# The shared expert of rows 11 to 15 run three steps later, with its input held in emptied staging memory

## The chip, the cores and the metric

The kernel runs on one core of a Trainium2 chip. The metric is the time of one execution in microseconds (us), by the device. Five engines share the core: TensorE (PE in the profile; its weight loads are PEld), VectorE (DVE), ScalarE (ACT), GpSimd (POOL) and SyncE (SP), which here only issues DMAs. Each runs its own list of instructions strictly in the order in which the program wrote it; they meet through semaphores.

## The reference, cut to what matters

The input is 16 rows of 128 tokens with 256 features, and a context of the same shape. Three blocks follow one another, each after a layer norm, each added to its input:

```python
x = x + attention(layernorm(x))                  # 16 heads of 16, rotary, causal
x = x + long_convolution(layernorm(x), ctx)      # 16 kernels as Toeplitz products, gated
x = x + moe(layernorm(x))
# moe: 16 experts of width 176, the best 4 of each token weighted by their softmax;
#      beside them one shared expert of width 704 for every token:
shared = silu(x @ Wg.T) * (x @ Wu.T) @ Wd.T * sigmoid(x @ gate_vec.T)
```

## The kernel before

**Two parts.** In the first part, `NB` = 16 rows go through a software pipeline: attention, convolution, router, choice of slots and shared expert. In it each token's normed input is scattered by four indirect DMAs (POOL, L1518) to the slots of its four experts, in device memory. In the second part, the slot stage, 79 tiles of 128 slots each are loaded, multiplied by their expert's weights (L762, L773, L785, L800) and stored; POOL gathers each token's four results and DVE adds them to the sum that the shared expert left.

**The order.** `ORDER` is written out by hand: for each engine, a list of pieces with how many steps each lies behind. In step s an engine runs, for every piece in its list's order, row s minus that number. On PE a step begins with `px` (the prefix sums that place the slots, behind 5, L640) and ends with `Tk`. `LAST` = 20 is the step in which row 15 gets its slots; in it DVE and POOL take the slot pieces first (`LAST_FIRST`).

**The shared expert's pieces**, by engine. PE: `ga0`, `ga1`, `up0`, `up1` (gate and up products, six matmuls of 352 columns each, L655; `ga0` is behind 4, the others 5), `Th0`, `Th1` (three transposes each, L665) and `dn` (18 matmuls, L677). ACT: `th0`, `th1` (tanh, L943) and `hh0`, `hh1` (L951). DVE: `s10`, `s11` (L1259), `s20`, `s21` (L1269), `hl0`, `hl1` (L1276) and `fin` (L1285), which adds the row's input `x2`. SP stores the sum (`store_shared`, L396). They read the row's normed input transposed, `xT`, and `x2`, both in rings of two buffers.

**Other pieces that the prediction names.** PE: `pt0` to `pt3` (transposes of the probabilities, L540), `at0` to `at3` (probabilities times values, L552), `cv0` to `cv3` (Toeplitz products, L585 and L589), `t2`, `t3`, `t4` (transposes; `t4`, L605, gathers the convolution's parts), `wo`. DVE: `mx` (row maxima, L1085), `gm` (gating of the convolution, L1122), `r1` (L1106). POOL: `kv` and `kl` (products of value and context, and their low half, L1467 and L1479), roots of the layer norms (L1439), scatters.

**Between the parts.** Three small products on PE turn the slot counts into a table of each tile's expert (`table_after`, after `px`, `Th1` and `dn` of step 20). PE then waits for all weights, runs 16 matmuls on zeros (`keep_busy(16, 7)`, L725), waits for the table, and takes the first tile. SP waits for the scatters and then loads eight tiles ahead (L451), after the last `store_shared`.

**Memory and banks.** The eight PSUM banks are used in the fixed turns of `PSUM_ORDER`; `free` waits for the reader of the use before. The weights pass through `stage`, a ring of three units of 1,024 columns, and are split there into high and low half (`PREPARE`, `PREPARE_LO`: the last unit in step 15); in the slot stage the same memory holds results.

Of the kernel before, what the change touches and what calls it, by code (L numbers as in the profile page):

```python
# [6 lines left out]
ALU = mybir.AluOpType  # L7
# [53 lines left out]
DEPTH = 8  # L61
# [54 lines left out]
def build(nc, x, ctx_in, w_units, w_route, bias, skip, trig, causal, ident, masks, ecol, iota, out):  # L116
    stack = ExitStack()
    with stack:
# [85 lines left out]
        cws = ring("shared_weight", 2, [P, 1])  # L204
# [48 lines left out]
        bhh = [st[:, 2240 + n * E:2240 + (n + 1) * E] for n in range(2)]  # L253

# [83 lines left out]

        def free(pe, use, row):

            b, i = HOME[use]
            line = BANKS[b]
            step = row + int(line[i][1])
            for back in range(1, 3 * len(line) + 1):
                n = i - back
                u, behind = line[n % len(line)]
                r = step + n // len(line) - int(behind)
                if 0 <= r < NB:
                    sig, k = READER[u]
                    sig.wait(pe, r, k)  # L350
                    return
                if step + n // len(line) < 0:
                    return
# [30 lines left out]
        def _(sp):  # L384
# [90 lines left out]
        def _(pe):  # L475
# [141 lines left out]
            def router(row):  # L617
                xT_lo.wait(pe, row)
                if row == 0:
                    pe.wait_ge(s_const_lo, 1)  # L620
                free(pe, "ro", row)
                n = 0
                for kc in range(KC):
                    for a in range(2):
                        for b in range(2):
                            last = nc.tensor.matmul(bank("ro")[:, 0:NR], xT[a][row % 2][:, kc, :], wr[b][:, kc, :],
                                                    start=n == 0, stop=n == 7)
                            n += 1
                last.then_inc(routed.sem, 1)
# [17 lines left out]
            def half_product(c, side, use, ready):  # L647
                def piece(row):
                    xT_lo.wait(pe, row)
                    if row == 0:  # L650
                        pe.wait_ge(s_w_lo, U_GU)
                    free(pe, use, row)
                    for kc in range(KC):
                        for a, b, first, end in products(kc == 0, kc == KC - 1):
                            last = nc.tensor.matmul(bank(use)[:, 0:CH], xT[a][row % 2][:, kc, :],  # L655
                                                    sgu[b][:, c, kc, side, :], start=first, stop=end)
                    last.then_inc(ready.sem, 1)
                return piece
# [73 lines left out]
            for s in range(NB + DEPTH):  # L732
                if s == 1:
                    pe.wait_ge(s_once, 4)
                for name, behind in ORDER["PE"]:
                    if 0 <= s - behind < NB:
                        pieces[name](s - behind)
                    if s - behind == NB - 1 and name in table_after:
# [11 lines left out]
            emptied(7)  # L750
            keep_busy(16, 7)
# [60 lines left out]
        def _(act):  # L812
# [102 lines left out]
            def moe_x_hi(row):  # L915
                xn3_T.wait(act, row)
                up_ready.wait(act, row - 2)
                nc.scalar.activation(xT[0][row % 2][:].rearrange("p c n -> p (c n)"), bank("xT")[:, 0:E], ACT.Copy)\
                    .then_inc(xT_hi.sem, 1)
# [40 lines left out]
            def first_use(row):  # L960
# [10 lines left out]
                "vT": copy_vT, "nm3": normalise(2, lambda row: x2[row % 2], scattered), "xh": moe_x_hi,  # L971
# [6 lines left out]
            for s in range(NB + DEPTH):  # L978
                if s == 1:
                    act.wait_ge(s_const, NCONST)  # L980
                    nc.scalar.activation(wr[0][:], wr_f[:], ACT.Copy, scale=WS).then_inc(s_const_hi, 1)
                    act.wait_ge(s_bias, 32)
                    nc.scalar.activation(brow[:], stage[:, RING - 1, :], ACT.Copy, scale=WS).then_inc(s_const_hi, 1)
                for n, (name, behind) in enumerate(ORDER["ACT"]):
                    for u in PREPARE.get((s, n), ()):
                        split_unit(u)
                    if 0 <= s - behind < NB:
                        pieces[name](s - behind)
# [35 lines left out]
        def _(dve):  # L1024
# [101 lines left out]
            def residual2(row):  # L1126
                o2_T.wait(dve, row)
                normed[2].wait(dve, row - 2)
                xsh_ready.wait(dve, row - 2)
                nc.vector.scalar_tensor_tensor(out=x2[row % 2][:], in0=bank("o2T")[:, 0:E], scalar=1.0 / WS,  # L1130
                                               in1=x1[row % 2][:], op0=ALU.mult, op1=ALU.add).then_inc(x2_ready.sem, 1)

            def moe_x_lo(row):
                xT_hi.wait(dve, row)
                nc.vector.tensor_tensor(xT[1][row % 2][:].rearrange("p c n -> p (c n)"), bank("xT")[:, 0:E],
                                        xT[0][row % 2][:].rearrange("p c n -> p (c n)"), ALU.subtract)\
                    .then_inc(xT_lo.sem, 1)

            def shared_weight(row):
                gth_done.wait(dve, row)  # L1140
                nc.vector.tensor_scalar(cws[row % 2][:], gth[row % 2][:], 1.0, 0.5 * SILU, ALU.add, ALU.mult)\
# [121 lines left out]
            def shared_up(c):  # L1263
                def piece(row):
# [4 lines left out]
                    nc.vector.scalar_tensor_tensor(out=hh[c][:, 0:CH], in0=bank(f"up{c}")[:, 0:CH], scalar=cws[row % 2][:],  # L1269
# [11 lines left out]
            def shared_out(row):  # L1281
                down_done.wait(dve, row)
                if row >= 2:
                    dve.wait_ge(s_xsh[row % 2], 16 * (row // 2))
                nc.vector.scalar_tensor_tensor(out=xsh[row % 2][:], in0=bank("dn")[:, 0:E], scalar=1.0 / WS,  # L1285
                                               in1=x2[row % 2][:], op0=ALU.mult, op1=ALU.add).then_inc(xsh_ready.sem, 1)
# [40 lines left out]
            table_after = {"ix": round_tiles, "hl1": mark_tiles, "fin": copy_table}  # L1327
            s_set = sem("buffers_set")
            for n in range(2):
# [18 lines left out]
                       (lambda row: x2[row % 2], lambda row: x2_ready.wait(dve, row)))  # L1348
# [7 lines left out]
            for s in range(NB + DEPTH):  # L1356
# [14 lines left out]
                for n, (name, behind) in enumerate(order("DVE", s)):  # L1371
                    for u in PREPARE_LO.get((s, n), ()):
                        split_unit(u)
                    if 0 <= s - behind < NB:
                        pieces[name](s - behind)
                    if s - behind == NB - 1 and name in table_after:
                        table_after[name]()
# [56 lines left out]
        def _(pool):  # L1434
# [117 lines left out]

            conv_ready.wait(pool, NB - 1)
# [103 lines left out]
```

## Time and profile before

| | |
|---|---|
| Time, median of 3 runs | 626.28 us (625.69 to 627.07) |
| Span of the profiled execution (first to last instruction) | 671.6 us |
| Mean granted clock of TensorE in it | 0.975 |
| Busy in the span: PE, DVE, ACT, POOL | 89%, 74%, 62%, 59% |

The profiled execution's own time is known only by its span, which is 45 us above the median of the runs without the profiler. An instruction counts as busy from its start to its end; matmuls overlap, and their ends are modelled, so a PE that is busy all through a stretch need not be at its peak in it. The granted clock is 1.00 at 2.4 GHz and 0.50 at 1.2 GHz. In the first part a step of the steady pipeline takes about 24.4 us. In the profile's time, step 16 begins on PE at 359.32, step 17 at 383.70, step 18 at 407.40, step 19 at 424.36 and step 20 at 433.88; the slot stage's first transpose starts at 450.59.

### The profile page before, as it was taken

The numbers are of one execution on the slowest core, as the hardware profiler recorded it, in microseconds if no ns is written. First come the engines' busy times: TensorE is split into PE (matmuls) and PEld (weight loads), VectorE is DVE, ScalarE is ACT, GpSimd is POOL, SyncE is SP. The second block draws the span as 40 slices with busy tenths as digits, with TensorE's granted clock in tenths as the row PEclk, the third lists the DMA queues.
The fourth block names the chain that finished last, engine by engine and source line by source line (L and its number), as shares of the span: only waits on it lengthen the run. The fifth ranks groups of instructions, "written<-read, shape, count | busy, mean of one in ns | idle before, by whom it ended". The sixth has DMA issues, their size and how long they took to land.

```text
span 671.6 us, 18614 instructions
## 1 busy us (share of the span) xinstructions
PE 597.1 (89%) x5901; PEld 464.0 (69%) x5901; DVE 495.8 (74%) x1516; ACT 414.5 (62%) x1060; POOL 394.7 (59%) x439
## 2 busy tenths in 40 slices
PE   8888999999999999999999998869998787878670
PEld 3567877888988878988988886636765455556450
DVE  4567797898898888998778667557766666767672
ACT  3877886787687687787677563216655454545440
POOL 1156768788888778778888778530023434343442
PEclk9999999999999999999999989979998989989996
DMA  6825422324432422532112100234455646555442
GB/s 181 288 86 174 144 74 86 124 75 135 128 91 85 126 77 100 158 96 89 38 52 79 50 12 31 72 117 126 128 141 155 180 146 185 166 178 166 147 125 90
DMA packets 55680, 78.93 MB, mean 118 GB/s; under 512 B 7330, under 2 KB 46370, under 8 KB 55588
## 3 DMA queue, kind: packets, MB, share of 16 engines
q1 hardware_dynamic: 37300, 48.51, 23.9%
q0 software_dynamic: 6912, 18.88, 9.3%
q10 hardware_dynamic: 11376, 10.36, 4.5%
q8 instruction: 52, 0.85, 0.5%
q14 instruction: 40, 0.33, 0.2%
HBM read 44.43 MB, written 33.29 MB: 116 GB/s over the span
## 4 chain that ended last, share of the span: by engine, by line
PE 73%; issue 8%; POOL 5%; ACT 4%; DVE 3%; another core or an unknown queue 2%; DMA 1%; ACTq 1%; SPq 1%; POOLq 0%; DVEq 0%
PE ps L773 10%; PE ps L655 8%; PE ps L552 7%; PE ps L585 5%; PE ps L486 5%; PE ps L677 5%; PE ps L785 4%; PE ps L605 4%; PE ps L796 3%; PE ps L540 3%; PE ps L589 3%; PE ps L762 2%; PE ps L523 2%; PE ps L513 2%
## 5 line engine op out<-in xcount | busy, mean ns | idle before, releaser
L1549 POOL DMA_INDIRECT toeplitz_lo<-y_slots,slots x44 | 42.4, 963 | 111.6 <-DMA y_slots<-stage 71.8
L773 PE MATMUL ps<-w_gate_up_hi,toeplitz_hi 128*128 x316 | 85.7, 319 | 14.6 <-DVE toeplitz_hi L1388 14.6
L1479 POOL TENSOR_TENSOR kv_lo<-kv,kv_hi 128x512 f16<-128x512 f32 x64 | 77.6, 1212 | 30.6 <-ACT kv_hi L911 30.3
L1518 POOL DMA_INDIRECT x_slots<-x_norm,slots x64 | 70.5, 1102 | 19.7 <-issue 14.9
L1467 POOL TENSOR_TENSOR kv<-ctx_t_sb,v_t 128x512 f32<-128x512 f32 x64 | 68.9, 1086 | 11.9 <-ACT v_t L900 9.5
L880 ACT ACTIVATE probs<-ps,row_neg_max 128x128 f32<-128x128 f32 x256 | 71.6, 390 | 3.4 <-DVE row_neg_max L1085 3.3
L552 PEld LDWEIGHTS ps<-v_ones,probs_t 128*128 128x128 f32 x512 | 62.2, 192 | 2.2
L1388 DVE TENSOR_TENSOR toeplitz_hi<-ps,toeplitz_hi 128x256 f16<-128x256 f32 x79 | 33.4, 423 | 40.1 <-ACT toeplitz_hi L994 38.8
L552 PE MATMUL ps<-v_ones,probs_t 128*128 128x17 f32 x512 | 60.7, 256 | 0.0
L585 PE MATMUL ps<-kv_hi,toeplitz_hi 128*128 128x128 f16 x256 | 56.6, 221 | 3.4 <-POOL kv_lo L1479 1.8
L994 ACT ACTIVATE toeplitz_hi<-ps 128x256 f16<-128x256 f32 x79 | 30.3, 383 | 45.3 <-ACT stage L1013 15.1
L1439 POOL TENSOR_TENSOR ln_rstd<-ln_var,minus_half 128x1 f32<-128x1 f32 x48 | 30.4, 634 | 46.7 <-DVE ln_var L1040 46.6
L585 PE MATMUL ps<-kv_hi,toeplitz_lo 128*128 128x128 f16 x256 | 56.4, 220 | 0.0
L585 PE MATMUL ps<-kv_lo,toeplitz_hi 128*128 128x128 f16 x256 | 56.4, 220 | 0.0
L1122 DVE TENSOR_TENSOR conv_gated<-ps,ctx_t_sb 128x512 f32<-128x512 f32 x64 | 43.7, 683 | 15.3 <-PE ps L589 15.0
L773 PEld LDWEIGHTS ps<-w_gate_up_hi,toeplitz_hi 128*128 128x128 f16 x316 | 31.3, 99 | 29.4 <-issue 17.4
L773 PE MATMUL ps<-w_gate_up_lo,toeplitz_hi 128*128 x158 | 50.2, 318 | 0.0
L589 PE MATMUL ps<-kv_hi,toeplitz_lo 128*128 128x64 f16 x256 | 49.6, 194 | 0.0
L589 PE MATMUL ps<-kv_lo,toeplitz_hi 128*128 128x64 f16 x256 | 49.6, 194 | 0.0
L589 PE MATMUL ps<-kv_hi,toeplitz_hi 128*128 128x64 f16 x256 | 49.6, 194 | 0.0
L1085 DVE TENSOR_REDUCE row_neg_max<-ps 128x4 f32<-128x512 f32 x64 | 43.2, 681 | 6.5 <-PE ps L529 6.5
L911 ACT ACTIVATE kv_hi<-kv 128x512 f16<-128x512 f32 x64 | 40.1, 626 | 9.7 <-PE ps L589 6.9
(226 smaller groups left out, 2099.1 us busy)
## 6 DMA issues: line engine op xcount, KB each, us to landing
stage<-in_w_units SPq DMA_DIRECT2D x36, 512.0 KB, 3.7
x_slots<-zeros SPq DMA_DIRECT2D x15, 512.0 KB
toeplitz_hi<-x_slots SPq DMA_DIRECT2D x40, 128.0 KB, 2.3
y_slots<-stage ACTq DMA_DIRECT2D x40, 128.0 KB, 2.3
y_slots<-kv ACTq DMA_DIRECT2D x39, 128.0 KB, 2.1
kv_hi<-x_slots SPq DMA_DIRECT2D x20, 128.0 KB, 2.7
x_slots<-zeros SPq DMA_DIRECT2D x1, 2432.0 KB
kv_lo<-x_slots SPq DMA_DIRECT2D x19, 128.0 KB, 2.2
```

Of the source, the lines that this page charges most:

```text
L552: last = nc.tensor.matmul(bank("av")[:, h * (HD + 1):(h + 1) * (HD + 1)], pT[g % 2][:, s, :], v_sb[row % 2][:, h, :], start=True, stop=Tru ...
L585: nc.tensor.matmul(to, toep_w[a][:, QUADS * g + h, 0, :], kvh[b][g % 2][:, h, :, :].rearrange("p c n -> p (c n)"), start=first, stop=end, ...
L589: last = nc.tensor.matmul(to[:, 64:128], toep_w[a][:, QUADS * g + h, 1, :], kvh[b][g % 2][:, h, 0, :], start=first, stop=end, skip_group_c ...
L655: last = nc.tensor.matmul(bank(use)[:, 0:CH], xT[a][row % 2][:, kc, :], sgu[b][:, c, kc, side, :], start=first, stop=end)
L773: last = nc.tensor.matmul(psum[2 + t % 2][:, 0:2 * INTER], bxT[a][t % 2][:, kc, :], egu[b][:, bass.ds(e, 1), kc, :].rearrange("p a n -> p ...
L880: last = nc.scalar.activation(sm[g % 2][:, s, :], bank(f"sc{g}")[:, s * P:(s + 1) * P], ACT.Exp, bias=mx[row % 2][:, g, s:s + 1])
L1085: nc.vector.tensor_reduce(mx[row % 2][:, g, :], bank(f"sc{g}")[:].rearrange("p (s n) -> p s n", n=P), X, ALU.max, negate=True).then_inc(ma ...
L1122: nc.vector.tensor_tensor(to, y, cT.broadcast_to([P, QUADS, KC, SIDE, SIDE]), ALU.mult)\
L1467: nc.gpsimd.tensor_tensor(kv[g % 2][:], cs.broadcast_to([P, SIDE, SIDE, SIDE]), vs.broadcast_to([P, SIDE, SIDE, SIDE]), ALU.mult).then_inc ...
L1479: nc.gpsimd.tensor_tensor(flat(kvh[1][g % 2]), kv[g % 2][:].rearrange("p h j i -> p (h j i)"), flat(kvh[0][g % 2]), ALU.subtract).then_inc ...
L1518: pool.indirect_dma_start(out=xbuf, out_offset=bass.IndirectOffsetOnAxis(ap=slots[:, row, j:j + 1], axis=0), in_=xn[2][row % 2][:], in_off ...
L1549: pool.indirect_dma_start(out=yg[n][j], out_offset=None, in_=ybuf[0:(last_tile(row) + 1) * P], in_offset=bass.IndirectOffsetOnAxis(ap=slot ...
```

## The change

Rows 0 to 10 stay as they were. The shared pieces of rows 11 to 15 run three steps later than their place in the lists gives: for a piece that lies b behind, steps b+11 to b+13 have none, and steps b+14 to b+18 take rows 11 to 15. The loop gets two more steps, in which (steps 21 to 23 on PE) only shared pieces of rows 13 to 15 are left. Their inputs are kept until then: `x2` and `xT` of those rows are written into `stage`, 512 columns a row. The 16 matmuls on zeros go.

```diff
-DEPTH = 8
+DEPTH = 10
+HELD, HOLD = 11, 3
+SHARED_PIECES = frozenset("ga0 ga1 up0 up1 Th0 Th1 ih0 ih1 dn th0 th1 hh0 hh1 s10 s11 s20 s21 hl0 hl1 fin store_shared".split())
+def due(name, behind, step):
+    row = step - behind
+    if name not in SHARED_PIECES or row < HELD:
+        return row
+    return row - HOLD if row >= HELD + HOLD else -1
...
-        cws = ring("shared_weight", 2, [P, 1])
+        cws = ring("shared_weight", 8, [P, 1])
...
+        def held(row, lo, hi):
+            at = 2 * E * (row - HELD)
+            return st[:, at + lo:at + hi]
+        def x2_of(row):
+            return x2[row % 2][:] if row < HELD else held(row, 0, E)
+        def xT_of(half, row):
+            if row < HELD:
+                return xT[half][row % 2][:]
+            return held(row, E + P * half, E + P * (half + 1)).bitcast(F16).rearrange("p (c n) -> p c n", c=KC)
+        def held_free(eng, row):
+            eng.wait_ge(s_w_lo, UNITS - RING + 1 + 2 * E * (row - HELD) // UNIT)
...
+        TURNS = [sorted((step, i, u, due(u, int(behind), step)) for i, (u, behind) in enumerate(line)
+                        for step in range(NB + DEPTH) if 0 <= due(u, int(behind), step) < NB) for line in BANKS]
+        BEFORE = {now[2:]: last[2:] for turns in TURNS for last, now in zip(turns, turns[1:])}
         def free(pe, use, row):
...
+            if (use, row) in BEFORE:
+                u, r = BEFORE[use, row]
+                sig, k = READER[u]
+                sig.wait(pe, r, k)
...
-                    row = s - behind
-                    if 0 <= row < NB and not (name == "load_x" and row < 3) and not (name == "load_ctx" and row < 2):
+                    row = due(name, behind, s)
+                    if 0 <= row < NB and not (name == "load_x" and row < 3) and not (name == "load_ctx" and row < 2) \
+                            and not (name == "store_shared" and row >= HELD + 2):
                         pieces[name](row)
...
             for t in range(NX):
                 load_tile(t)
+            for row in range(HELD + 2, NB):
+                store_shared(row)
...
             pe.wait_ge(s_w_lo, UNITS)
-            emptied(7)
-            keep_busy(16, 7)
             pe.wait_ge(s_table, 1)
...
             def moe_x_hi(row):
                 xn3_T.wait(act, row)
-                up_ready.wait(act, row - 2)
+                if row < HELD:
+                    up_ready.wait(act, row - 2)
+                else:
+                    held_free(act, row)
...
             def gate_th(t):
                 t_gu.wait(act, t)
                 t_ga.wait(act, t - 2)
+                if t == 0:
+                    up_ready.wait(act, NB - 1)
+                    xsh_ready.wait(act, NB - 1)
...
             def residual2(row):
                 o2_T.wait(dve, row)
-                normed[2].wait(dve, row - 2)
-                xsh_ready.wait(dve, row - 2)
+                if row < HELD:
+                    normed[2].wait(dve, row - 2)
+                    xsh_ready.wait(dve, row - 2)
+                else:
+                    held_free(dve, row)
...
-            table_after = {"ix": round_tiles, "hl1": mark_tiles, "fin": copy_table}
+            table_after = {(LAST, "ix"): round_tiles, (LAST, "hl1"): mark_tiles, (LAST + 1, "fin"): copy_table}
...
+            xsh_ready.wait(pool, NB - 1)
             conv_ready.wait(pool, NB - 1)
```

Every other edited line passes the row through `due`, `x2_of` or `xT_of`; on PE the three products of the table stay in step 20.

## Rows read from the trace of the kernel before

**Rows 1.** The page: the span, and the chain that ended last, by engine.

```profile
span 671.6 us, 18614 instructions
...
PE 73%; issue 8%; POOL 5%; ACT 4%; DVE 3%; another core or an unknown queue 2%; DMA 1%; ACTq 1%; SPq 1%; POOLq 0%; DVEq 0%
```

**Rows 2.** Windows: length, busy us of PE, PEld, DVE, ACT, POOL; granted clock, DMA.

```profile
359.32:383.70 24.38, 24.38 (x290) 20.72 (x287) 17.76 (x59) 16.77 (x44) 19.41 (x22) 1.00 0.18 60
383.70:407.40 23.70, 23.69 (x267) 20.19 (x265) 16.44 (x52) 14.35 (x39) 16.19 (x20) 0.93 0.11 34
407.40:424.36 16.96, 13.66 (x180) 11.21 (x177) 11.66 (x40) 5.86 (x14) 15.34 (x19) 1.00 0.10 36
424.36:433.88 9.52, 7.52 (x66) 5.11 (x63) 7.11 (x33) 3.28 (x9) 4.66 (x7) 1.00 0.21 71
433.88:447.13 13.25, 8.77 (x57) 5.95 (x55) 6.82 (x34) 1.64 (x4) 5.71 (x8) 0.74 0.20 71
447.13:450.59 3.46, 3.46 (x18) 1.62 (x17) 1.56 (x9) 0.00 (x0) 0.94 (x2) 1.00 0.49 159
...
480.00:500.00 20.00, 20.00 (x151) 14.19 (x150) 14.41 (x51) 13.29 (x40) 1.87 (x2) 1.00 0.47 129
```

**Rows 3.** Timeline of PE: start us, us, line, shapes; around the shared products.

```profile
366.19 0.53 PE L665 MATMUL ps<-identity,inner 128*128 128x128 f32 x3
...
434.11 0.31 PE L655 MATMUL ps<-w_shared_gate_up_hi,moe_x_t_hi 128*128 128x352 f16 x1
...
436.64 0.31 PE L655 MATMUL ps<-w_shared_gate_up_hi,moe_x_t_lo 128*128 128x352 f16 x1
...
450.59 0.38 PE L762 MATMUL ps<-identity,toeplitz_hi 128*128 128x128 f32 x2
```

**Rows 4.** Chain of waits: start us, us, what; `dn` of rows 13, 15.

```profile
420.56 1.97 PE ps L677 x18
...
443.01 4.02 PE ps L677 x18
```

**Rows 5.** Timelines of DVE and POOL, steps 17, 18; in brackets the idle before.

```profile
386.86 0.51 DVE L1259 SCALAR_TENSOR_TENSOR gate_th<-gate_th,ps 128x352 f32<-128x352 f32 x1
387.29 1.28 DVE L1085 TENSOR_REDUCE row_neg_max<-ps 128x4 f32<-128x512 f32 x2
...
398.68 0.26 DVE L1092 RECIPROCAL softmax_recip<-ps 128x16 f32<-128x16 f32 x1 [1.66 <-PE ps L552]
...
403.47 0.41 DVE L1106 SCALAR_TENSOR_TENSOR x<-ps,x_sb 128x256 f32<-128x256 f32 x1
...
420.65 0.69 DVE L1122 TENSOR_TENSOR conv_gated<-ps,ctx_t_sb 128x512 f32<-128x512 f32 x1 [1.19 <-PE ps L589]
...
404.84 0.57 POOL L1439 TENSOR_TENSOR ln_rstd<-ln_var,minus_half 128x1 f32<-128x1 f32 x1 [0.36 <-DVE ln_var L1040]
...
408.20 2.09 POOL L1467 TENSOR_TENSOR kv<-ctx_t_sb,v_t 128x512 f32<-128x512 f32 x2 [0.27 <-issue]
```

**Rows 6.** POOL's groups, 360 to 420 us: busy, mean ns | idle before, releaser.

```profile
L1479 POOL TENSOR_TENSOR kv_lo<-kv,kv_hi 128x512 f16<-128x512 f32 x12 | 13.8, 1151 | 7.9 <-ACT kv_hi L911 7.9
L1467 POOL TENSOR_TENSOR kv<-ctx_t_sb,v_t 128x512 f32<-128x512 f32 x12 | 12.6, 1061 | 1.0 <-issue 0.5 <-ACT v_t L900 0.5
L1518 POOL DMA_INDIRECT x_slots<-x_norm,slots x9 | 9.7, 1074 | 2.3 <-issue 2.3
...
L1506 POOL TENSOR_TENSOR slot_weight_of<-slot_hit,expert_weight 128x64 f32<-128x64 f32 x2 | 0.6, 320 | 1.9 <-issue 1.8
```

**Rows 7.** Timelines of ACT, DVE and SP from step 20 on.

```profile
441.24 0.49 ACT L951 ACTIVATE inner_t_hi<-ps 128x384 f16<-128x384 f32 x1 [4.39 <-issue]
...
439.66 1.07 DVE L1269 SCALAR_TENSOR_TENSOR inner<-ps,shared_weight,gate_th 128x352 f32<-128x352 f32 x2
...
441.76 1.20 DVE L1276 TENSOR_TENSOR inner_t_lo<-ps,inner_t_hi 128x384 f16<-128x384 f32 x2 [1.03 <-ACT inner_t_hi L951]
...
447.95 1.81 SPq L451 DMA_DIRECT2D toeplitz_hi<-x_slots  x4
```

More of the change, by code:

```diff
@@ L625, in router @@
                         for b in range(2):
-                            last = nc.tensor.matmul(bank("ro")[:, 0:NR], xT[a][row % 2][:, kc, :], wr[b][:, kc, :],
+                            last = nc.tensor.matmul(bank("ro")[:, 0:NR], xT_of(a, row)[:, kc, :], wr[b][:, kc, :],
                                                     start=n == 0, stop=n == 7)
@@ L654, in piece @@
                         for a, b, first, end in products(kc == 0, kc == KC - 1):
-                            last = nc.tensor.matmul(bank(use)[:, 0:CH], xT[a][row % 2][:, kc, :],
+                            last = nc.tensor.matmul(bank(use)[:, 0:CH], xT_of(a, row)[:, kc, :],
                                                     sgu[b][:, c, kc, side, :], start=first, stop=end)
@@ L735, in _ @@
                 for name, behind in ORDER["PE"]:
-                    if 0 <= s - behind < NB:
-                        pieces[name](s - behind)
-                    if s - behind == NB - 1 and name in table_after:
+                    if 0 <= due(name, behind, s) < NB:
+                        pieces[name](due(name, behind, s))
+                    if s == LAST and name in table_after:
                         table_after[name]()
@@ L916, in moe_x_hi @@
                 xn3_T.wait(act, row)
-                up_ready.wait(act, row - 2)
-                nc.scalar.activation(xT[0][row % 2][:].rearrange("p c n -> p (c n)"), bank("xT")[:, 0:E], ACT.Copy)\
+                if row < HELD:
+                    up_ready.wait(act, row - 2)
+                else:
+                    held_free(act, row)
+                nc.scalar.activation(xT_of(0, row).rearrange("p c n -> p (c n)"), bank("xT")[:, 0:E], ACT.Copy)\
                     .then_inc(xT_hi.sem, 1)
@@ L970, in _ @@
                 "hi2": lhs2, "nm2": normalise(1, lambda row: x1[row % 2], lambda row: v_T.wait(act, row - 1)),
[L971 removed]
+                "vT": copy_vT, "nm3": normalise(2, x2_of, scattered), "xh": moe_x_hi,
                 "gt": gate_tanh, "lg": logits, "re": router_exp,
@@ L986, in _ @@
                         split_unit(u)
-                    if 0 <= s - behind < NB:
-                        pieces[name](s - behind)
+                    if 0 <= due(name, behind, s) < NB:
+                        pieces[name](due(name, behind, s))
             def x_hi(t):
@@ L1140, in shared_weight @@
                 gth_done.wait(dve, row)
-                nc.vector.tensor_scalar(cws[row % 2][:], gth[row % 2][:], 1.0, 0.5 * SILU, ALU.add, ALU.mult)\
+                nc.vector.tensor_scalar(cws[row % 8][:], gth[row % 2][:], 1.0, 0.5 * SILU, ALU.add, ALU.mult)\
                     .then_inc(cws_done.sem, 1)
@@ L1268, in piece @@
                     inner_T.wait(dve, row - 1, c + 1)
-                    nc.vector.scalar_tensor_tensor(out=hh[c][:, 0:CH], in0=bank(f"up{c}")[:, 0:CH], scalar=cws[row % 2][:],
+                    nc.vector.scalar_tensor_tensor(out=hh[c][:, 0:CH], in0=bank(f"up{c}")[:, 0:CH], scalar=cws[row % 8][:],
                                                    in1=th[c][:], op0=ALU.mult, op1=ALU.mult).then_inc(inner_done.sem, 1)
@@ L1347, in _ @@
             sources = ((lambda row: x_sb[row % 3], x_ready), (lambda row: x1[row % 2], lambda row: x1_ready.wait(dve, row)),
-                       (lambda row: x2[row % 2], lambda row: x2_ready.wait(dve, row)))
+                       (x2_of, lambda row: x2_ready.wait(dve, row)))
             for n, (src, ready) in enumerate(sources):
@@ L1373, in _ @@
                         split_unit(u)
[L1374 to L1377, printed above, removed]
+                    if 0 <= due(name, behind, s) < NB:
+                        pieces[name](due(name, behind, s))
+                    if (s, name) in table_after:
+                        table_after[s, name]()
             for n in range(2):
```

21 lines of the change are left out of this document (4 added, 17 removed).

## The prediction

> **What bounds the kernel now.** I read the chain of waits first: 73% of the span is PE's [rows 1], so PE's time is the price of most things. Then windows cut where a step begins on PE. The first number behind the length is PE's busy time. In steps 16 and 17 PE is busy throughout (24.38 of 24.38, 23.69 of 23.70); in step 18 it is busy 13.66 of 16.96 while POOL has 15.34; in steps 19 and 20 nothing is full: PE has 7.52 of 9.52 and 8.77 of 13.25, the latter at a granted clock of 0.74 [rows 2]. The slot stage then has a PE busy for 20.00 of 20.00 again, so a late start of it is paid in full. From the first transpose at 450.59 [rows 3] to the end of the span lie 671.6 - 450.6 = 221 us that the change doesn't touch. So the question is one date: when does the slot stage start?
>
> A busy PE is not yet a bound. POOL has 19.41 of step 16's 24.38 us [rows 2], and most of what is left is its waiting [rows 6]. The pipeline runs close to two bounds; taking work off one lets it shorten only as far as the other.
>
> **What the moved work costs on PE.** 18 gate and up matmuls start between 434.11 and 436.64, 0.149 us apart [rows 3]; 24 a row make 3.6 us. Two groups of three transposes take 0.53 each with the tail of the last [rows 3], some 0.4 to the next instruction: 0.8. `dn` takes 1.97 [rows 4]. Together 6.3 us a row.
>
> **Steps 16 to 18: three rows' products leave.** If PE alone set the pace, 3 x 6.3 = 18.9 us would go. I follow the waits instead.
>
> Step 17: `s11` leaves DVE ahead of the row maxima (386.86, the maxima at 387.29 [rows 5]). The exponentials and `pt0` need the maxima, so `up0` and `up1`, which filled that wait, yield some 0.5, not 1.8. `Th0`, `Th1` between the transposes: 0.8. `ga0` lay beside the reciprocal, which waited 1.66 for PE [rows 5], and the output's normalisation: 0.5. `dn` lay beside the chain residual (403.47), root of the layer norm on POOL (404.84), two scatters, next products (408.20) [rows 5], which keeps its 4.7 us: nothing. At a clock of 0.93 [rows 2], 0.07 x 23.7 x 2 = 3.3 us ran at 1.2 GHz and cost at most half of that; with PE no longer the bound I take 1.2 as recovered. Sum 3.0.
>
> Step 16: 0.5 and 0.8 as above, nothing for `ga0` and the clock (1.00), and 0.8 for `dn`, which there outlasts the layer norm: 2.1. Step 18: POOL runs almost without a gap from 408.20 until row 15's last `kl`; 0.3 of waiting goes. `dn` (420.56, 1.97 [rows 4]) then lay between `cv3` and `t4`; but `t4` must wait for the gating (420.65, 0.69 [rows 5]), so 1.1 of it goes: 1.4.
>
> Sum of the gains: 2.1 + 3.0 + 1.4 = 6.5 us. Bound above: all waiting of POOL between 360 and 420 that others cause goes, 7.9 + 1.0 + 1.9 = 10.8 [rows 6] (the 2.3 between scatters follow their own issue and stay), and all of `dn`, 2.0: 12.8. Bound below: a loss of 1, if a thinner PE gets step 17's clock in step 16 too and nothing else moves. I take 6.5; the nearest row is step 18, where PE already had 3.3 us free and POOL set the length.
>
> **Steps 19 and 20: other rows, same work.** Rows 11 and 12 stand where 14 and 15 stood, in the same places of each list, also behind DVE's slot pieces in step 20. New is `ga0` of row 13 between the table's second product and `dn`: 0.9 us, 1.8 at 1.2 GHz (`dn` took 4.02 there instead of 1.97 [rows 4]), against some 1.1 in which `dn` (443.01 [rows 4]) waited for `hl1` (441.76 and 1.20 on [rows 7]): +0.7, bounds 0 and 1.8.
>
> **Steps 21 to 23: the three rows come back, ahead of the first tile.** PE is in order, so the first tile waits for `dn` of row 15. A row's cycle: `ga1`, `up0`, `up1` 2.7 us, with tanh (no row shows it here; as long as `hh`, 0.49 [rows 7]), `s11` 0.5 and `s20` beside them; `Th0`, then `Th1` behind `s21` (a pair takes 1.07 [rows 7]), at 3.9; the next row's `ga0` beside `hh1` 0.49 and `hl1` 0.6 [rows 7], at 5.1; `dn` 2.0: 7.1. Three rows: 21.3 us from the end of the table's products. Bound below: no idle, 3 x 6.3 less the `ga0` counted in step 20: 18.0. Above: step 19's pace, 9.5 [rows 2]: 28.5.
>
> What hides there: the 3.5 us from 447.13 to 450.59 [rows 2]. The 16 matmuls on zeros that go filled exactly those, but what PE waited for was data, the first tile's load being issued at 447.95 [rows 7]; so dropping them saves nothing beyond these 3.5. The loads land long before `dn` of row 15, which spares the first tiles' waits: 0.8 (bounds 0 and 1.5, estimated; no row of its own).
>
> **Waits and queues.** SP issues the stores of rows 11 and 12, then the eight loads, then three stores; `fin` of row 15 needs only row 13's store, done some 7 us before. `gate_th` of tile 0 now waits for `fin` of row 15, due half a us after `dn`; `gate_up` of that tile ends later; behind it in ACT's list stand tile 1's pieces, which need PE anyway. POOL's gathers queue behind a wait for the same `fin`, and need stored tiles, far later. `held_free` asks for weight units split by step 15, before row 13 needs them: nothing. Deeper `cws`, other addresses, fewer ring waits: nothing queued on those. If a cover fails, the stage starts later by that wait, at most 2 us.
>
> **Sum.** -6.5 + 0.7 + 21.3 - 3.5 - 0.8 = +11.2: the span goes from 671.6 to 682.8 us. The span is 45 us over the median of the runs shown; I don't know where that time lies, but the terms are lengths of the first part's work, so I put the difference on the median: 626.28 + 11.2 = 637.5 us.
>
> **The rivals.**
>
> *PE is the bound after all (faster).* For it: PE is busy 100% of steps 16 and 17. Then 18.9 go and the 1.2 of clock: -20.1 + 17.7 = -2.4, 623.9 us. The place is POOL: its waits for ACT's `kv_hi` [rows 6] would have to vanish and its own work shrink. It turns at a gain of 17.7, above the bound of 12.8. Chance 0.10.
>
> *POOL runs without waiting (slower by less).* -12.8 + 17.7 = +4.9, 631.2; with rows 13 to 15 dense as well (18.0), +1.6, 627.9. For it: PE is what `kv_hi` waits for in the end. Against: `kl3` waits for `pt3`, behind an exponential chain that stays. Chance 0.13; its lower end touches no change.
>
> *The clock falls in steps 16 to 18.* The granted clock was 0.93 in step 17 although PE was busy throughout, and 0.74 in step 20 [rows 2]. What leaves is plain matmuls; transposes stay. At 0.74 over the 65.0 - 6.5 = 58.5 us then left, 0.26 x 58.5 = 15.2 us of PE time are lost; PE has about that much idle there, so I put half on the path: +7.6, 645.1. The Trainium skill, "TensorE: Matmul & The Clock Gate", part 4 on the transpose mode, says that a transpose doesn't count as PE activity the way a matmul does; by it, step 17's dip with a full PE is what a step rich in transposes gives, and this rival gains weight. Against, by the rows: step 16 has the same transposes at 1.00. Chance 0.09.
>
> *Rows 13 to 15 take step 19's pace.* 28.5 instead of 21.3: +7.2, 644.7. For it: step 20 takes 13.25 for one row. Against: both steps hold the router's chain and slots, which these three lack. Chance 0.08.
>
> **How the numbers follow.** The forecast has 0.60, with its own range of 632 to 642 (gain 2 to 10, cycles of 6.7 to 7.6). About 0.2%, 1.25 us, is what a measurement tells from no change. Faster: 0.10, the first rival. Within 0.2%: 0.06, the second's dense end and what lies between the two. Slower: 0.84. The range 628 to 645 leaves out the first rival, the second's last edge and half of the last two: under 0.2.
>
> **What would show it.** In the profile after: step 16 about 22 us long, 17 about 20.5, 18 about 15.5, POOL's share in them up, PE's below 85%; row 15's `px` near 427.4; three groups of 24 L655, 6 L665 and 18 L677, about 7 us apart, before the first L762 near 461.8; no L725 there; the stage still 221 us. A first L762 at or before 450.6 makes the forecast wrong: then PE set steps 16 to 18. If it comes near 469, the clock or the last rows' waits were mis-sized.

## The result, and the profile after

The kernel after takes 647.85 us (median of 4 runs, 643.0 to 650.14), the kernel before in the same job 625.99 us (625.16 to 627.07): ratio 1.0363 [1.0324, 1.0402], 21.9 us slower. The forecast was slower by 11.2 us, with a range that ended at 645.

One thing must be put right before the profiles are compared. The execution of before that is shown ahead of the prediction was not like the others: its 671.6 us are 45 over the runs, and what disturbed it is not known. A second profile of before was therefore taken (first experiment), and in this part "before" is that profile wherever no group of rows is named. Windows of it, cut where row 11's to row 15's prefix product starts on PE and at the first transpose of the slot stage (length, busy us of PE, PEld, DVE, ACT, POOL, granted clock, DMA):

```profile
358.51:382.89 24.38, 24.38 (x290) 20.72 (x288) 17.74 (x58) 16.77 (x44) 18.89 (x22) 1.00 0.16 55
382.89:404.90 22.01, 22.01 (x266) 19.12 (x264) 15.46 (x53) 14.37 (x39) 16.03 (x20) 1.00 0.11 35
404.90:421.73 16.83, 13.68 (x180) 11.21 (x178) 12.54 (x41) 5.86 (x14) 15.29 (x19) 1.00 0.12 42
421.73:429.97 8.24, 7.26 (x66) 5.19 (x64) 6.85 (x32) 3.28 (x9) 4.58 (x7) 1.00 0.20 66
429.97:443.77 13.80, 10.01 (x73) 5.93 (x71) 8.32 (x42) 1.64 (x4) 6.68 (x10) 1.00 0.34 112
```

The same cuts in the kernel after, where the last window but one ends with the table's products and the last holds rows 13 to 15:

```profile
357.44:379.67 22.23, 19.21 (x241) 16.20 (x239) 14.89 (x51) 15.61 (x40) 18.07 (x21) 1.00 0.18 59
379.67:405.91 26.24, 21.18 (x219) 18.97 (x216) 15.39 (x46) 12.83 (x35) 16.27 (x19) 0.80 0.06 22
405.91:425.98 20.07, 13.00 (x137) 11.33 (x136) 11.84 (x35) 4.59 (x11) 15.71 (x19) 0.66 0.08 27
425.98:434.23 8.25, 7.27 (x66) 5.18 (x64) 6.85 (x32) 3.19 (x9) 4.72 (x7) 1.00 0.19 66
434.23:442.95 8.72, 7.20 (x63) 4.86 (x60) 7.03 (x34) 2.10 (x5) 5.70 (x8) 1.00 0.30 106
442.95:464.95 22.00, 19.22 (x141) 13.31 (x141) 11.29 (x26) 5.27 (x11) 0.32 (x1) 1.00 0.21 67
```

The chain of waits is PE's still, with 77% of the span (80% in before, 73% in the shown profile [rows 1]):

```profile
span 646.2 us, 18581 instructions
...
PE 77%; issue 6%; POOL 6%; DVE 4%; ACT 3%; DMA 2%; SPq 1%; POOLq 0%; DVEq 0%; ACTq 0%
```

The slot stage starts 21.18 us later (464.95 against 443.77) and then lasts as long as before (646.2 - 464.95 = 181.2; 625.2 - 443.77 = 181.4). So all of the loss is one date, as the prediction had it. It is made up of: -1.07 before step 16 (0.99 of it stands already at step 14, ahead of the first piece that was moved, so it parts the two executions and not the kernels), -2.15 in step 16, **+4.23 in step 17, +3.24 in step 18**, +0.01 in step 19, +16.92 from step 20's start to the stage. The end was forecast at +17.7. Steps 16 to 18 were to give 6.5 back and took 5.3 more.

The three rows at the end, PE's timeline (the first `dn` matmul of rows 13 and 14, the first transpose of the stage; compare [rows 3, 4]):

```profile
448.37 0.28 PE L702 MATMUL ps<-w_shared_down_hi,inner_t_hi 128*128 128x256 f16 x1 [0.28 <-DVE inner_t_lo L1308]
...
455.67 0.28 PE L702 MATMUL ps<-w_shared_down_hi,inner_t_hi 128*128 128x256 f16 x1 [0.28 <-DVE inner_t_lo L1308]
...
464.95 0.60 PE L785 MATMUL ps<-identity,toeplitz_hi 128*128 128x128 f32 x4
```

and in before, the matmuls on zeros and the first transpose of the stage:

```profile
438.78 3.63 PE L725 MATMUL ps<-zeros 128*128 128x512 f16 x16
443.77 0.41 PE L762 MATMUL ps<-identity,toeplitz_hi 128*128 128x128 f32 x2 [1.36 <-DMA toeplitz_hi<-x_slots]
```

A row's cycle is 7.30 us with 0.6 of idle, and the first tile's transpose no longer waits for its load, as it did for 1.36 us in before.

What stands in steps 17 and 18 is seen on DVE. The scan that numbers the tiles, 128 x 16 elements, in the kernel after (start, us, engine, line, operation; first step 17, then step 18):

```profile
380.41 3.67 DVE L1234 TENSOR_TENSOR_SCAN tile_newest<-ones_f,tile_newest,tile_opened 128x16 f32<-128x16 f32 x1
...
384.41 0.68 DVE L1114 TENSOR_REDUCE row_neg_max<-ps 128x4 f32<-128x512 f32 x1
...
406.64 3.85 DVE L1234 TENSOR_TENSOR_SCAN tile_newest<-ones_f,tile_newest,tile_opened 128x16 f32<-128x16 f32 x1
```

and POOL beside it:

```profile
380.81 2.10 POOL L1499 TENSOR_TENSOR kv<-ctx_t_sb,v_t 128x512 f32<-128x512 f32 x2
382.86 1.16 POOL L1511 TENSOR_TENSOR kv_lo<-kv,kv_hi 128x512 f16<-128x512 f32 x1
384.43 0.57 POOL L1471 TENSOR_TENSOR ln_rstd<-ln_var,minus_half 128x1 f32<-128x1 f32 x1 [0.41 <-DVE ln_var L1069]
...
407.24 2.10 POOL L1499 TENSOR_TENSOR kv<-ctx_t_sb,v_t 128x512 f32<-128x512 f32 x2
409.29 1.15 POOL L1511 TENSOR_TENSOR kv_lo<-kv,kv_hi 128x512 f16<-128x512 f32 x1
```

In before the scan of step 17 took 0.24 us (that of step 18 0.99):

```profile
383.62 0.24 DVE L1202 TENSOR_TENSOR_SCAN tile_newest<-ones_f,tile_newest,tile_opened 128x16 f32<-128x16 f32 x1
...
383.89 1.00 DVE L1207 TENSOR_TENSOR tile_ahead<-tile_newest,tile_end 128x16 f32<-128x16 f32 x1
...
383.80 2.09 POOL L1467 TENSOR_TENSOR kv<-ctx_t_sb,v_t 128x512 f32<-128x512 f32 x2 [0.69 <-ACT v_t L900]
385.86 1.14 POOL L1479 TENSOR_TENSOR kv_lo<-kv,kv_hi 128x512 f16<-128x512 f32 x1
```

Read the ends. The scan after ends at 384.08 and 410.49, just when POOL's unbroken run of kv, kv, kv_lo has ended (384.02, 410.44). POOL then stands still for 0.41 us, waiting for a layer norm piece that itself queued on DVE behind the scan. In before POOL waited 0.69 us for `v_t` first, and the scan slipped in at 383.62. One thing the records leave open: the held scans are recorded 0.40 and 0.60 us ahead of the first kv, and a free one, 0.23 us long, would have been over by then. What shut them out began before POOL's product is recorded. The row maxima queue behind the scan; PE's next transposes wait for them. The chain of waits has the scan on it, and PE's timeline shows the holes:

```profile
380.49 3.59 DVE tile_newest L1234
```

```profile
386.42 0.45 PE L565 MATMUL ps<-identity,probs 128*128 128x128 f32 x1 [2.81 <-ACT probs L903]
...
410.50 0.29 PE L610 MATMUL ps<-kv_hi,toeplitz_hi 128*128 128x128 f16 x1 [4.32 <-POOL kv_lo L1511]
```

The granted clock goes to 0.50 in these holes, which is 1.2 GHz of 2.4, and PE's work runs at that pace for 10.2 and 13.7 us:

```profile
385.54:395.78 10.24, 9.37 (x90) 9.33 (x91) 4.03 (x13) 6.03 (x19) 5.34 (x7) 0.50 0.00 1
409.43:423.08 13.65, 10.62 (x112) 9.11 (x112) 6.46 (x19) 3.52 (x9) 10.88 (x13) 0.50 0.03 11
```

The second hole is not the scan's: PE waits there for POOL's `kv_lo`. In before 18 gate and up matmuls (2.84 us) lay in it and 1.17 us of idle was left.

### The profile page after: what moved, and what is told of

Its sections match the earlier page's. It is cut to its first block, busy times and chain, and to the rows that moved or that the text cites. A ratio compares the mean times of both kernels' runs of the same rounds, so it can differ in the third digit from the quotient of the medians.

```text
span 646.2 us, 18581 instructions
## 1 busy us (share of the span) xinstructions
PE 592.7 (92%) x5885; PEld 465.1 (72%) x5885; DVE 499.4 (77%) x1516; ACT 417.4 (65%) x1060; POOL 396.8 (61%) x439
## 4 chain that ended last, share of the span: by engine, by line
PE 77%; issue 6%; POOL 6%; DVE 4%; ACT 3%; DMA 2%; SPq 1%; POOLq 0%; DVEq 0%; ACTq 0%
PE ps L796 11%; PE ps L680 9%; PE ps L577 7%; PE ps L610 6%; PE ps L702 5%; PE ps L511 5%; PE ps L808 4%; PE ps L819 4%; PE ps L565 4%; PE ps L630 3%; PE ps L614 3%; PE ps L785 3%; POOL kv_lo L1511 2%; PE ps L548 2%; PE ps L538 2%
## 5 line engine op out<-in xcount | busy, mean ns | idle before, releaser
L1511 POOL TENSOR_TENSOR kv_lo<-kv,kv_hi 128x512 f16<-128x512 f32 x64 | 80.4, 1257 | 35.5 <-ACT kv_hi L934 35.2
L796 PE MATMUL ps<-w_gate_up_hi,toeplitz_hi 128*128 x316 | 83.7, 313 | 1.0 <-DVE toeplitz_hi L1420 1.0
L1550 POOL DMA_INDIRECT x_slots<-x_norm,slots x64 | 69.0, 1077 | 19.1 <-issue 14.8
L610 PE MATMUL ps<-kv_hi,toeplitz_hi 128*128 128x128 f16 x256 | 58.4, 228 | 6.2 <-POOL kv_lo L1511 5.8
L610 PE MATMUL ps<-kv_hi,toeplitz_lo 128*128 128x128 f16 x256 | 58.7, 229 | 0.0
L610 PE MATMUL ps<-kv_lo,toeplitz_hi 128*128 128x128 f16 x256 | 58.7, 229 | 0.0
L614 PE MATMUL ps<-kv_hi,toeplitz_hi 128*128 128x64 f16 x256 | 51.2, 200 | 0.0
L915 ACT ACTIVATE probs_t<-ps 128x512 f32<-128x512 f32 x64 | 39.0, 613 | 10.9 <-PE ps L565 10.7
```

The lines of the kernel that those rows point to most:

```text
L610: nc.tensor.matmul(to, toep_w[a][:, QUADS * g + h, 0, :], kvh[b][g % 2][:, h, :, :].rearrange("p c n -> p (c n)"), start=first, stop=end, ...
L614: last = nc.tensor.matmul(to[:, 64:128], toep_w[a][:, QUADS * g + h, 1, :], kvh[b][g % 2][:, h, 0, :], start=first, stop=end, skip_group_c ...
L796: last = nc.tensor.matmul(psum[2 + t % 2][:, 0:2 * INTER], bxT[a][t % 2][:, kc, :], egu[b][:, bass.ds(e, 1), kc, :].rearrange("p a n -> p ...
L1511: nc.gpsimd.tensor_tensor(flat(kvh[1][g % 2]), kv[g % 2][:].rearrange("p h j i -> p (h j i)"), flat(kvh[0][g % 2]), ALU.subtract).then_inc ...
L1550: pool.indirect_dma_start(out=xbuf, out_offset=bass.IndirectOffsetOnAxis(ap=slots[:, row, j:j + 1], axis=0), in_=xn[2][row % 2][:], in_off ...
```

## The experiments

Three theories. **P**: DVE's small operations with two operands in SBUF are shut out while POOL's products run on; in steps 17 and 18 that makes PE late and idle. **C**: PE's clock falls because the shared products left. **B**: POOL or one row's chain sets these steps, so nothing was to be had. What all runs gave, in us of their one profile (cuts as above), and the time as a ratio to before, which was timed anew beside each group of runs. A profile is one execution; those of D, E and one row are of the fastest run of their kernel, that of D again of the slowest.

| kernel | 16 | 17 (clock) | 18 (clock) | less than before, 16 to 18 | ratio |
|---|---|---|---|---|---|
| before | 24.38 | 22.01 (1.00) | 16.83 (1.00) | | |
| after | 22.23 | 26.24 (0.80) | 20.07 (0.66) | -5.3 | 1.0363 [1.0324, 1.0402] |
| A, late kv0 | 22.23 | 23.62 (0.86) | 17.18 (0.80) | +0.2 | 1.0274 [1.0216, 1.0332] |
| B, filler | 23.44 | 23.28 (0.93) | 20.04 (0.74) | -3.5 | 1.0349 [1.0311, 1.0387] |
| D, scan in PSUM | 22.23 | 20.17 (1.00) | 17.25 (0.80) | +3.6 | 1.0248 [1.0215, 1.0281] |
| D again | 23.41 | 23.36 (0.85) | 17.27 (0.80) | -0.8 | 1.0273 [1.0242, 1.0305] |
| E, D and filler | 22.23 | 20.64 (1.00) | 18.02 (0.91) | +2.3 | 1.0270 [1.0236, 1.0305] |
| G, D and hole filled | 22.23 | 20.18 (1.00) | 19.85 (0.83) | +1.0 | 1.0252 [1.0224, 1.0279] |
| one row | 22.31 | 23.81 (1.00) | 16.82 (1.00) | +0.3 | 1.0088 [1.0053, 1.0122] |
| one row, scan in PSUM | 22.31 | 21.91 (1.00) | 16.83 (1.00) | +2.2 | 1.0034 [1.0011, 1.0058] |

**The kernel before, again** (no edit).

> The kernel before once more, for a second profile of it. In the profile shown the slot stage lasted 221 us, in the kernel after 181.2 us (465.0 to 646.2), though the change leaves that stage alone. If the profile of before was disturbed there, its stage now takes 172 to 182 us and the first transpose of it again lies near 450.6. A stage near 174 would mean that some 7 us of the 21.9 lost lie in the stage itself; a stage near 181 would mean that the first part of the kernel before is shorter than its profile showed, by some 7 us.

Measured: span 625.2, stage 181.4, first transpose at 443.77. So the stage is as long as after's, and the shown profile was too long in its first part as well, by 6.8 us: 1.7 in step 17, 1.3 in step 19, 2.9 from step 20 on, in a stretch with a granted clock of 0.74 [rows 2], where `dn` took 4.02 us [rows 4] against 2.15 here, 0.8 before step 16 and 0.1 in step 18.

**A: POOL's first products later.**

```
 # POOL, first value products of a row
+if row in (14, 15):
+    page_step.wait(pool, row - 2, 3)      # scan and lookup of the row two before are done
```

> The kernel after, but POOL begins the value products of rows 14 and 15 only when DVE has done the scan and the tile lookup of the row two before. Theory P (the scan, 3.67 and 3.85 us instead of 0.23, is held by POOL's unbroken run of products; PE then stands idle, and its clock falls for that): the scan takes 0.2 to 1 us in steps 17 and 18, the granted clock there is 0.9 or more, and the time falls by 8 to 12 us against the kernel after, to 636 to 640. Theory C (the clock falls because plain matmuls left these steps, whatever the scan does): the scans are short but the clock stays at 0.80 and 0.66, and the time falls by 3 us at most. Theory B (POOL or the chain of one row sets the length of these steps in any case): scans short, clock up, time down by less than 3.

```profile
380.46 0.23 DVE L1234 TENSOR_TENSOR_SCAN tile_newest<-ones_f,tile_newest,tile_opened 128x16 f32<-128x16 f32 x1
...
385.06 0.41 PE L565 MATMUL ps<-identity,probs 128*128 128x128 f32 x2 [1.16 <-ACT probs L903]
...
408.01 0.29 PE L610 MATMUL ps<-kv_hi,toeplitz_hi 128*128 128x128 f16 x1 [4.39 <-POOL kv_lo L1513]
...
404.98 0.87 DVE L1264 SCALAR_TENSOR_TENSOR slot_key<-picked,slot_place 128x16 f32<-128x16 f32 x1
```

The scans are short (0.23 in both steps), PE's wait in step 17 falls from 2.81 to 1.16, and steps 17 and 18 give back 2.62 and 2.89 us. But the clock still falls, at 385.79, and steps 17 and 18 run at 0.86 and 0.80. POOL's products begin only 0.3 us later for it (381.13 against 380.81 in the same step). The time is 643.60 us; the ratio goes down by 0.9%, 5.6 us, between what P and C expected: the hold is real, and it isn't all. This run is also the nearest to one without holds: no DVE operation of its steps 16 to 18 takes over 1.13 us (`slot_key` 0.87). Yet steps 16 to 18 give 0.2 us in its profile where 6.5 were forecast.

**B: the clock alone.** In steps 16 to 18 PE multiplies zeros where the shared products stood.

```
+FILL = {"up1": 10, "ga0": 2, "dn": 3}    # matmuls on zeros, s in (16, 17, 18)
+elif name in FILL and s in (16, 17, 18):
+    fill(name, s)
```

> The kernel after, but in steps 16 to 18 PE does matmuls on zeros where the shared products stood (10 at the place of up1, 2 of ga0, 3 of dn), whose results nobody reads. Theory C (the clock falls for want of plain matmuls): clock back at 0.95 to 1.00 in steps 17 and 18, the time 5 to 8 us below the kernel after. Theory P: the scans still last 3.6 us, clock up in part, the time down by 4 us or less. Theory B: no change within 1.5 us either way.

```profile
382.81 3.67 DVE L1244 TENSOR_TENSOR_SCAN tile_newest<-ones_f,tile_newest,tile_opened 128x16 f32<-128x16 f32 x1
...
382.08:405.36 23.28, 21.51 (x233) 17.14 (x231) 15.84 (x46) 12.58 (x35) 16.29 (x19) 0.93 0.07 24
405.36:425.40 20.04, 14.89 (x150) 11.46 (x149) 12.81 (x35) 4.59 (x11) 15.69 (x19) 0.74 0.08 28
```

The clock comes back in part, the scan stays held, step 17 gains 3.0, step 16 loses 1.2 to the filler, and the time, 647.17 us, does not move outside its interval; C's 5 to 8 us are missed; theories P and B had both allowed for this. Filling in zeros alone is not the way out.

**D: the hold alone.** For rows 12 and 13 the scan reads its second operand from PSUM and writes there, and the lookup reads it there; POOL's work stays where it was.

```
# shortened
+tensor_scalar(px[:, 48:64], px[:, 0:16], ...)             # the opened tiles, in PSUM too
-tensor_tensor_scan(newest, ones_f, opens, start, ...)     # both inputs in SBUF
+tensor_tensor_scan(px[:, 64:80], ones_f, px[:, 48:64], start, ...)
-tensor_tensor(ahead, newest, tile_end, subtract)
+tensor_copy(newest, px[:, 64:80]); tensor_tensor(ahead, px[:, 64:80], tile_end, subtract)
```

> The kernel after, but for rows 12 and 13 the scan takes its opened tiles from PSUM and leaves its result there, and the tile lookup reads it there, so that each has one operand in SBUF instead of two; POOL's work is not moved. If POOL's products shut these two out because both of their operands lie in SBUF, the scan takes 0.3 us at most in steps 17 and 18 and the lookup too, PE's idle of 2.81 and 4.32 us shrinks, step 17 comes to 23 to 24 us and step 18 to 16 to 17.2, and the time falls by 4 to 7 us against the kernel after, to 641 to 644; a clock that still falls in step 17 would then be a second, separate cost (theory C). If the scan was late for another reason (its semaphores, DVE's queue), it still takes some 3.7 us and nothing changes.

```profile
379.74 0.24 DVE L1239 TENSOR_TENSOR_SCAN ps<-ones_f,tile_newest,ps 128x16 f32<-128x16 f32 x1
...
380.10 0.16 DVE L1252 TENSOR_TENSOR tile_ahead<-ps,tile_end 128x16 f32<-128x16 f32 x1
...
380.06 2.10 POOL L1512 TENSOR_TENSOR kv<-ctx_t_sb,v_t 128x512 f32<-128x512 f32 x2
...
400.88 2.78 DVE L1277 SCALAR_TENSOR_TENSOR slot_key<-picked,slot_place 128x16 f32<-128x16 f32 x1
...
378.92:399.09 20.17, 16.77 (x219) 14.61 (x217) 11.84 (x48) 12.48 (x35) 16.27 (x19) 1.00 0.08 28
399.09:416.34 17.25, 10.62 (x138) 9.43 (x137) 10.97 (x37) 4.59 (x11) 15.19 (x19) 0.80 0.09 31
```

This is P's answer. With POOL's work where it was, the scan takes 0.24 instead of 3.67 us. It is over (379.98) before kv is recorded (380.06), so by itself it shows only that it was not shut out. The lookup runs within kv: 0.16 us with one input in PSUM, where it took 1.00 in before with both in SBUF. Its result still goes to SBUF, so for the lookup it is the input that counts; of the scan both an input and the result were moved. Step 17 falls to 20.17, where the prediction had put it (20.5): against before's 22.01 that is a gain of 1.84, and the forecast without its 1.2 for the clock was 1.8. The Trainium skill states the rule in "SBUF — State Buffer", "Who interferes with whom": a DVE instruction with two SBUF inputs contends with a GpSimd instruction that reads SBUF; one with a single SBUF input doesn't, outside the modes that use both ports. These rows agree with it. The lookup's 1.00 us in before, to the end of the first of POOL's two kv, agrees too. The hold over three POOL instructions (3.67 us) is longer than the one instruction that the Trainium skill speaks of.

What stays is the next operation of the same kind: `slot_key`, both inputs in SBUF, is held 2.78 us in step 18. That hold costs nothing that shows: in A `slot_key` took 0.87 us and the step 17.18, here 17.25. And PE's hole of 4.31 us before `cv0` is still there (the expectation had it shrink), with the clock at half from 402.25. The time, 641.16 us, is the one expected.

**One row instead of three**, without and with the scan in PSUM.

```
-HELD, HOLD = 11, 3
+HELD, HOLD = 11, 1
```

> The kernel after with the shared expert one step later instead of three: one row instead of three stands behind the table, and the steps in the middle keep their products but for the first one moved. By the lengths measured in the kernel after, one row at the end costs 22.05 / 3 = 7.35 us instead of 22.05, less the 3.5 us in which the first tile's load is waited for, less some 2 us from step 20: about +1.4 against the kernel before, 627 to 628, if the steps in the middle give nothing back; if the loss sits in the steps 16 to 18 as such (theory C), the one step that is thinned loses its clock as well and it comes out at 629 to 631.

> The kernel with the shared expert one step later instead of three, and the scan and lookup of rows 12 and 13 with one operand in SBUF. In the run with one row its step 17 took 23.81 us with the scan at 3.66 us, against 22.01 in the kernel before with 0.24; step 16 took 22.31 against 24.38, and the end 16.14 against 13.80. With the scan free step 17 should take 22.0, which makes 0.7 us less than the kernel before: 624 to 626. If the scan's hold was harmless there (PE is full in that step), it stays at 628 to 631.

Step 17 and its scan, first without, then with the edit of D:

```profile
380.26 3.66 DVE L1234 TENSOR_TENSOR_SCAN tile_newest<-ones_f,tile_newest,tile_opened 128x16 f32<-128x16 f32 x1
...
379.53:403.34 23.81, 22.12 (x267) 19.07 (x264) 17.62 (x53) 14.04 (x39) 16.80 (x20) 1.00 0.08 28
```

```profile
382.17 0.24 DVE L1239 TENSOR_TENSOR_SCAN ps<-ones_f,tile_newest,ps 128x16 f32<-128x16 f32 x1
...
381.36:403.27 21.91, 21.91 (x266) 19.20 (x264) 16.23 (x55) 14.01 (x39) 16.82 (x20) 1.00 0.09 31
```

Here the clock is 1.00 in both and the shared products are back in step 17, so this pair shows the hold by itself: 1.9 us of step 17. It also fits what sets it off. Step 16 lost its products in both, came out 2 us shorter, and in step 17 POOL began its products without the wait for `v_t`. The first version came to 630.14 us, which the expectation had put down to C; its profile, of the fastest of its four runs, shows no fall of the clock in these steps, but the held scan. The version with the scan free was meant to beat the kernel before, at 624 to 626; with 627.48, 1.0034 [1.0011, 1.0058], it is slower by about 2 us. One row costs 2.6 us at the end (24.67 against 22.04 us from step 19's start to the stage) and gives 2.2 in steps 16 to 18.

**E and G: the scan free, and PE kept busy.** E puts 8 and 10 zero matmuls at `up1`, 2 and 6 at `ga0`, 3 and 8 at `dn` in steps 17 and 18; G only 5 and 14 at `up1`, where PE stood idle.

```
+FILL = {17: {"up1": 8, "ga0": 2, "dn": 3}, 18: {"up1": 10, "ga0": 6, "dn": 8}}   # E
+FILL = {17: {"up1": 5}, 18: {"up1": 14}}                                         # G
```

> The same with the scan and lookup free of SBUF's second operand, and in steps 17 and 18 PE also does matmuls on zeros (8 and 10 at the place of up1, 2 and 6 of ga0, 3 and 8 of dn) that nobody reads. If the held scan and the clock are two costs that add up (26.2 to 23.6 us in step 17 by the one, to 23.3 by the other), step 17 comes to 20.6 us at a granted clock of 1.00 and step 18 to 16 to 17.2, and the time is 8 to 10 us under the kernel after, 638 to 640: the prediction's terms, with step 18 short by its POOL. If POOL or a row's chain bounds these steps anyway (theory B), step 17 stays above 22.5 us and the time within 2 us of the run with the scan alone.

> The kernel after with the scan and lookup freed as before, and matmuls on zeros only where PE stands idle: 5 in step 17 and 14 in step 18 at the place of up1, some 1.1 and 3.0 us of the idle 1.9 and 4.31 us; nobody reads them. In the run with the scan alone PE's clock fell in that hole of step 18 (half from 402.25 to 409.08 us), ACT then waited 3.13 us for PE's transposes with kv_hi queued behind, and the step took 17.25 us. If the clock falls because PE stands idle there, it stays at 1.00 now and step 18 takes 15.7 to 16.3 us, the 15.5 of the prediction nearly; the time is 1 to 3 us under that run's. If it falls because plain matmuls are fewer over the whole step, or if POOL sets the step at any clock, step 18 stays at 16.8 us or more and the time where it is.

POOL, DVE and PE in step 18 of G, and its window:

```profile
406.03 2.27 POOL L1534 TENSOR_TENSOR kv_lo<-kv,kv_hi 128x512 f16<-128x512 f32 x2
...
406.47 3.57 DVE L1281 SCALAR_TENSOR_TENSOR tile_end<-tile_fresh,tile_end 128x16 f16<-128x16 f32 x1
409.97 0.68 DVE L1162 TENSOR_TENSOR conv_gated<-ps,ctx_t_sb 128x512 f32<-128x512 f32 x1
...
411.88 0.18 PE L652 MATMUL ps<-w_route_hi,stage 128*128 128x17 f16 x1 [2.08 <-DVE stage L1178]
...
399.96:419.81 19.85, 14.22 (x152) 11.36 (x151) 13.19 (x37) 4.59 (x11) 16.65 (x20) 0.83 0.10 35
```

G's expectation of 15.7 to 16.3 us for step 18 missed by 4; its time is 641.48 us, inside D's interval. Filling the hole did keep the clock at 1.00 there (it falls only at 412.92, after the wait of 2.08). But with PE on time POOL's two next kv_lo follow without a gap, and `tile_end`, which in D fell into that gap (0.16 us at 406.50), is held for 3.57 us: it has two SBUF inputs as well. Behind it stand the gating and the residual sum that PE needs. E shows the same hold (3.56); there step 17 came to its 20.6, step 18 to 18.02 instead of 16 to 17.2, and the time to 642.19 instead of 638 to 640. So filling PE works on the clock, and the hold takes the gain back.

**D again.**

> The kernel with the scan and lookup freed, once more, beside the run with the hole filled. 638 to 643 us as before. If its granted clock in step 17 falls in this profile, step 17 takes some 23.6 us instead of 20.17, which would be what parts its slower runs (641 to 643) from the fastest (638).

```profile
359.73:383.14 23.41, 20.49 (x242) 17.51 (x240) 14.91 (x51) 15.59 (x40) 17.79 (x20) 0.93 0.16 52
383.14:406.50 23.36, 19.96 (x218) 17.80 (x216) 11.71 (x48) 12.58 (x35) 16.22 (x19) 0.85 0.07 24
```

The same kernel, the same wait of 1.15 us ahead of the probabilities' transposes in step 17, and here the clock falls behind it (389.21 to 396.04) where it held in the first profile: 23.36 against 20.17 us. The time is 643.52 us, half a us over what was expected. So beside the hold there is a cost of the clock, some 3 us in step 17, that the thinned step does not pay in every run. Step 16 paid too here, 1.2 us, for a fall of 3.4 us (375.56 to 378.98) behind a wait of 0.61.

What tips the clock, the runs do not show. In steps 16 to 18 of the kernels with three rows moved, every fall of 6.8 us or more began inside a PE wait of 1.15 us or more, or within 1.1 us behind one. But waits of 1.15 us (D, step 17) and 1.68 us (one row, step 17) passed without a fall. And falls of 3.4 us came with no wait over 0.3 us in the 9 us before them: at 399.14 in the shown profile, where PE was full, and at 398.50 in B. Step 18 is plainer: the clock fell in it in all seven profiles without the 18 gate and up matmuls near its start, with fillers or not, and in none of the four with them.

## Why the prediction was wrong

The direction was right, and so was the reading that all of the loss is one date. The end of the kernel was nearly right too: three rows took 22.00 us where 21.3 were forecast (a row 7.3 instead of 7.1). `ga0` of row 13 cost nothing instead of 0.7 (8.72 us from step 20's start to the end of the table's products, 8.81 in before), zeros and load hid 4.99 us instead of 3.5, and the stage, which was to save 0.8 of waits, kept its length: together 16.92 instead of 17.7, with errors that went both ways. Step 16 gave 2.15; the forecast was 2.1. Step 19 kept its length, and the table's steps ran at full clock.

**The step that failed is the gain of steps 17 and 18**: 3.0 and 1.4 in the forecast, -4.2 and -3.2 measured. With step 16 the loss is 5.3 us, past the bound below (a loss of 1) as well. Three things were wrong in it.

- It followed the waits with every duration held at its row of before. In the trace of the shown profile the scan takes 0.73 and 0.39 us in these steps and from 0.23 to 1.03 in the others, the lookup 0.96 to 0.98 in steps 14 to 18 and 0.17 in steps 19 and 20, where no products of POOL stand: a duration that varies like this can be a sign of a shared resource. The prediction passed over these rows and asked only which piece waits for which. Freeing scan and lookup takes 1.15 and 0.90% off the ratio (D's two runs against after), 7.2 and 5.6 us with some 3 us of uncertainty each, of the 10.4 by which the time lies above the forecast; A, by another way, takes off 5.6.
- It took the clock as something that comes back when PE is less full (1.2 us recovered). The dip of step 17 in the shown profile [rows 2] is not there in the second profile of before, so there was nothing to recover. And a less full PE lost its clock. The rival "the clock falls in steps 16 to 18" came near the size, 645.1, at a chance of 0.09, but it did not have the hold. Its reason, that plain matmuls leave and transposes stay, holds for step 18 at most: step 16 keeps 1.00 with the same transposes and no shared products in every profile but D again (0.93), and step 17 kept it in D, E and G.
- In step 18 it counted that 1.1 us of `dn` would go, and they went (from the end of cv3's products to the next transposes 1.8 us in before, 0.8 in D). The 18 gate and up matmuls got no price there, because POOL set the length; they lay in the 4.3 us in which PE waits for `kv_lo`, and without them the clock fell in every run (in G, with the wait filled, later in the step). In D the step came to 17.25 us, not under 16.83. That POOL or a row's chain bounds this step in any case (theory B) is not excluded: no run had it under 16.82.

In step 17 the shares can be estimated from the profiles: 20.17 us without either (D), 23.36 and 23.62 with the clock's fall alone (D again, A), 26.24 with both (after). So some 3.3 us are the clock's and some 2.7 the hold's (1.9 in the pair with one row), which also made the fall longer (10.2 us against 6.8). In step 18 they can't be parted, because a PE that is on time moves DVE into the next hold. That without any hold the sum would have come out at +11.2 is not shown, and A, with nothing held long, speaks against it. A run that keeps PE filled in step 18 and frees `tile_end` too is missing.

The base was also at fault by its own account: the 45 us between the profile and the runs were noted and set aside. Two terms read from it (0.93 in step 17, 0.74 in step 20) belonged to that execution, and so did the stage of 221 us, which took 181.2.

## What to carry to other kernels

When a step is thinned on one engine, list the small operations of the others that share a resource with a third, and look for one whose duration already varies between steps: what was interleaved by luck moves into a long run of its rival. Work that fills a wait is not free to remove only because the wait stays; here the clock fell in step 18 of every run without it. Before a base is taken from one profile, hold it against the runs, and if it is off by more than the effect, don't price terms that only that execution shows.

## What the runs showed of the hardware

A DVE scan on 128 x 16 elements took 3.67 us instead of 0.24 when POOL's products followed its scatter at once, and 0.24 again with an operand and the result in PSUM; a lookup of that size took 1.00 us within kv with both inputs in SBUF and 0.16 within kv with one. Such an operation was let in after one POOL instruction in some places (the lookup's 1.00 us in before), and only after three or more in others (3.67; 3.57 across two kv_lo, kv and a skip product in G). A scatter of POOL alone did not hold it: in A the scan took 0.23 us at 380.46, beside a scatter from 379.89 to 380.85. A fall of the clock of 3.4 us in step 15 made that step 26.0 us instead of 24.4 (B, D again, E). In neither of the two profiles of before does any DVE operation of steps 16 to 18 wait like that for over 1.2 us; in eight of the nine other profiles at least one does.
